# State products moved ahead of the diagonal and carried blocks of a Mamba-2 layer, and VectorE's weighting of x ahead of its gate

## The reference, cut to what matters

```python
states = jnp.einsum('bclh,bclhn,bclhp->bchpn', decay_states * dt_c, B_c, x_c)
def step(prev, inp):
    st, cd = inp
    new = cd[:, :, None, None] * prev + st
    return (new, prev)
Y_off = jnp.einsum('bclhn,bchpn,bclh->bclhp', C_c, prev_states, state_decay_out)
yh = (Y_diag + Y_off).reshape(b, l, H, P) + D_param[None, None, :, None] * x
hidden = yr * jax.nn.silu(gate)
hidden = hidden * lax.rsqrt(var + EPS) * norm_w
return hidden @ out_proj_w
```

## Time and profile before

| | |
|---|---|
| three runs | 1876.63, 1875.66, 1876.63 us, median 1876.63 |
| profiled execution | 1876.75 us, of which 1875.0 us from the first to the last instruction |
| busy share of the span | TensorE 99%, VectorE 80%, ScalarE 66%, GpSimd 44% |
| granted TensorE clock, mean | 0.999 of full speed |
| pair stage | four times some 230 us, between the attention parts |

### The profile page before, as it was taken

One profiled execution on the slowest core, in us unless ns is written; L12 is line 12 of the kernel. 1 busy time (PEld: TensorE's weight loads), 2 busy tenths in 40 slices (PEclk: granted clock), 3 DMA queues, 4 the chain that ended last, 5 costly groups with the idle time before them and its releaser, 6 DMA issues.

```text
span 1875.0 us, 42153 instructions
## 1 busy us (share of the span) xinstructions
PE 1852.3 (99%) x12602; PEld 1574.3 (84%) x12602; DVE 1500.1 (80%) x2736; ACT 1237.9 (66%) x2867; POOL 828.0 (44%) x1005
## 2 busy tenths in 40 slices
PE   8999999999999999999999999999999999999998
PEld 7888778888888878888888887888888888788886
DVE  6886778888788468888888846988888883688886
ACT  5663489999455247888755525888865551588885
POOL 2210379998200027777710002777770000277776
PEclk9999999999999999999999999999999999999999
DMA  6330478887422125656622212656652321366663
GB/s 242 126 126 1 158 231 264 259 265 240 144 78 89 54 82 194 209 205 218 210 98 79 77 54 82 227 205 206 217 189 90 91 66 54 117 215 205 207 215 112
DMA packets 157193, 290.76 MB, mean 155 GB/s; under 512 B 12944, under 2 KB 83792, under 8 KB 157008
## 3 DMA queue, kind: packets, MB, share of 16 engines
q1 hardware_dynamic: 157136, 290.04, 46.6%
HBM read 248.70 MB, written 38.14 MB: 153 GB/s over the span
## 4 chain that ended last, share of the span: by engine, by line
PE 92%; DVE 3%; ACT 2%; issue 1%; POOL 1%; DMA 0%; SPq 0%; POOLq 0%; DVEq 0%; ACTq 0%
PE bank L745 40%; PE bank L1047 11%; PE bank L1034 7%; PE bank L1014 6%; PE both L745 5%; PE bank L863 4%; PE bank L1023 4%; PE bank L1006 3%; PE bank L912 2%; PE bank L831 1%; PE bank L837 1%; PE both L863 1%; PE bank L753 1%; PE bank L750 1%; PE bank L751 1%
## 5 line engine op out<-in xcount | busy, mean ns | idle before, releaser
L745 PE MATMUL bank<-xn_r,w_r 128*128 128x512 f32 x2268 | 566.6, 398 | 0.9 <-DVE xn_r L1738 0.9
L745 PEld LDWEIGHTS bank<-xn_r,w_r 128*128 128x128 f32 x2268 | 412.6, 188 | 83.6 <-issue 1.1
L1510 DVE SCALAR_TENSOR_TENSOR conv_acc<-bank,conv_sb,conv_acc 128x511 f32<-128x511 f32 (+2 forms) x408 | 304.0, 745 | 44.7 <-DVE conv_acc L1510 17.3
L605 POOL TENSOR_TENSOR rstd<-var_eps,minus_half 128x4 f32<-128x4 f32 (+2 forms) x12 | 9.7, 807 | 603.8 <-DVE var_eps L1439 603.8
L1047 PE MATMUL bank<-wo_n,place 128*128 128x256 f32 x1024 | 242.4, 380 | 2.3 <-DVE place L1687 2.3
L626 POOL TENSOR_TENSOR c_grow<-c_grow,c_t 128x768 f32<-128x768 f32 x128 | 234.0, 1828 | 22.5 <-DVE place L1519 22.5
L1159 ACT ACTIVATE place_r<-bank 128x512 fp32r<-128x512 f32 (+1 forms) x320 | 158.7, 556 | 120.6 <-PE bank L745 96.0
L1426 DVE TENSOR_TENSOR place_r<-bank,place_r 128x512 fp32r<-128x512 f32 (+1 forms) x320 | 186.3, 630 | 63.6 <-ACT place_r L1159 63.6
L1047 PEld LDWEIGHTS bank<-wo_n,place 128*128 128x128 f32 x1024 | 184.8, 190 | 22.8 <-DVE place L1687 2.7
L648 POOL TENSOR_TENSOR sumsq<-sumsq,place 128x512 f32<-128x512 f32 x127 | 162.0, 1276 | 17.0 <-ACT place L1227 17.0
L1238 ACT ACTIVATE conv_acc<-bank,conv_sb 128x512 f32<-128x512 f32 x136 | 105.7, 778 | 89.2 <-PE bank L745 85.3
(11 more groups left out here) (174 smaller groups left out, 3544.8 us busy)
## 6 DMA issues: line engine op xcount, KB each, us to landing
place_r<-cum_rows SPq DMA_DIRECT2D x128, 512.0 KB, 4.3
c_grow<-grow_rows SPq DMA_DIRECT2D x128, 384.0 KB, 3.5
w_r<-pair_split SPq DMA_DIRECT2D x96, 512.0 KB, 3.7
w_r<-qkv_split SPq DMA_DIRECT2D x48, 512.0 KB, 4.0
pair_split<-w_r SPq DMA_DIRECT2D x32, 512.0 KB, 3.4
qkv_split<-w_r SPq DMA_DIRECT2D x16, 768.0 KB, 3.9
w_r<-qkv_split SPq DMA_DIRECT2D x48, 256.0 KB, 3.2
wo_n<-out_split SPq DMA_DIRECT2D x96, 128.0 KB, 2.0
```

Source lines behind the costliest of these rows:

```text
L745: ins = mm(out, lhsT=w(a), rhs=m(b), start=(start and i == 0), stop=(stop and i == 2), **kw)
L1510: stt(out=conv_acc[:, back:W], in0=src[:, 0:W - back], scalar=conv_sb[:, ch, TAPS - 1 - back:TAPS - back], in1=conv_acc[:, back:W], op0=AL ...
```

## The change

On TensorE, make_states(n+1) moves from the end of the pair to right behind project_out(n-1), so that in_block(n) and off_block(n) come last. On VectorE, weighted(n+1) is issued before pair_gate(n+1). ScalarE, GpSimd and SP keep their orders, and no semaphore or buffer changes.

```diff
                     if before > 0:
                         project_out(b, n - 1, 1 - par, isinstance(n, int) and n == 1, False)
+                    if more:
+                        make_states(b, n + 1, 1 - par)
                     in_block(b, n, par)
                     off_block(b, n, par)
-                    if more:
-                        make_states(b, n + 1, 1 - par)
...
                     mixed(b, n, par)
                     if more:
+                        weighted(b, n + 1, 1 - par)
                         pair_gate(b, n + 1, 1 - par)
-                        weighted(b, n + 1, 1 - par)
                         if ahead:
                             conv_taps(K + n + 4, n + 2 if isinstance(n, int) else bass.ds(n + 2, 1), bank[1])
```

## The result

| | before | after |
|---|---|---|
| median | 1876.62 us | 1936.55 us (1934.61 to 1936.92) |
| ratio | | 1.0319, 95% interval 1.0302 to 1.0335 |
| span of the profiled execution | 1875.0 us | 1935.1 us |
| mean granted clock | 0.999 | 0.999 |
| looped pair, mean distance of in_block's starts, 1720 to 1840 us | 7.487 us | 7.949 us |

What follows compares the result with a forecast made beforehand. TensorE was taken as the bound, with nothing waiting in the loop. 120 looped pairs at +0.45 us (54.0), first pairs 6.5 and the end 0.7 add 61.2 to 1876.75: 1938 us, 3.3% slower, range 1903 to 1970.

Steps and rivals of the forecast that it cites:

- The state products would stand for weigh_x: In looped pairs behind project_out, TensorE would idle about 0.5 us before the state products' weight loads.
- L: Hand-over latencies from turn_x through weighted and weigh_x to the state products: 0.35 us a pair, bounds 0.12 and 0.55.
- operands picked by a register: In the loops, instructions picking columns by register can start later; turn_x to weighted taken as 0.11 us, bounds 0.03 and 0.2.
- W: Gaps at tile changes, state products to in_block 0.24 us and off_block to next gate projection 0.17: 0.41, bounds 0 and 0.73.
- the rule L + W - 0.31: Change in us per looped pair: +0.45 forecast, -0.19 with low bounds, +0.97 with high ones.
- worth up to 0.16 us a pair to the new order: At tile changes on TensorE, the price goes with the preceding matmul, favouring the new order by up to 0.16 us a pair.
- Free tile changes: Rival: tile changes cost nothing in the new places, +0.04 us a pair, about 1887 us (1880 to 1912); chance 0.12.
- The rival on the other side: Rival: the chain hides after all and the shorter gap stays as gain, 1859 us at -0.19 a pair; chance 0.04.
- A second late party: Rival: conv_end, mixed or ScalarE late, or gaps and latencies at upper ends; +0.75 to +0.97 a pair, 1976 to 2002; chance 0.10.
- The granted clock: Rival: TensorE's clock falls to 1.2 GHz because it stands 0.5 us each pair, about 2040 us; chance 0.03.
- pair 0: First pair of each sequence, no output projection before the state products, chain bare: +1.63 us, four times, 6.5 us.
- the end: In the last sequence the last output projections wait for gated behind the final off_block: +0.7 us.

Runs made afterwards that it cites:

- experiment 4: Changed kernel, but state products read x weighted by dt alone, decay to the chunk's end left out, so nobody waits for weigh_x; 1877.69 us, ratio 1.0008.
- turn_late: Against the kernel before: turn_x moved behind project_out, state products still last, VectorE issuing weighted before pair_gate; 1922.57 us, ratio 1.0250.
- experiment 3: Changed kernel with the state products moved between in_block and off_block, VectorE as in the changed kernel; 1918.11 us, ratio 1.0223.
- experiment 8: Against the kernel before: turn_x behind project_out, gate projection n+2 between off_block and the state products, VectorE in its old order; 1876.38 us, ratio 1.0002.
- Experiments 6 and 9: 6 is turn_late; 9 is experiment 8 with VectorE's weighted before pair_gate, 1922.72 us, ratio 1.0249.
- experiment 2: Against the kernel before: only TensorE's move, state products behind project_out, with pair_gate still before weighted on VectorE; 1983.2 us, ratio 1.0570.

## Why the prediction was right

**The state products would stand for weigh_x: right.** About 0.5 us forecast from the pair's own rows, 0.60 to 0.62 measured before the weight loads in looped pairs (0.58 in sequence 0); without anyone waiting for weigh_x the loss is gone (experiment 4). Three experiments changed the chain's length and the time followed (table above).

**The chain's terms: right, L slightly small.** L was taken as 0.35. In the pair shown it is 0.16 + 0.20 + 0.05 = 0.41. The chain from turn_x's end to the state products is 1.93 us, forecast 1.86. Where L comes from shows in pair 1, which is written out and not looped. There turn_x ends at 1684.77:

```profile
1684.81 0.69 DVE L1543 TENSOR_TENSOR place<-bank,dt_sb 128x512 f32<-128x512 f32 x1 [0.18 <-PE bank L1006]
...
1685.58 0.83 POOL L619 TENSOR_TENSOR shared<-place,dec 128x384 f32<-128x384 f32 x1 [0.33 <-DVE place L1543]
...
1686.46 0.74 PEld L1014 LDWEIGHTS bank<-shared,b_sb 128*128 128x128 f32 x6 [0.37 <-POOL shared L619]
```

The three hand-overs are 0.04, 0.08 and 0.05 us, 0.17 in all and 0.24 less than in the loop, and the state products stand 0.37 us instead of 0.61. VectorE is not what makes the first one longer in the loop: in turn_late, where it stands idle for 1.00 us, the hand-over is 0.17 too (1792.03 to 1792.20). So being in the loop adds 0.24 us a pair to this chain, in its first two hand-overs. The prediction's reason, operands picked by a register, fits, but nothing here isolates it. For the first hand-over the prediction took 0.11, between the 0.03 outside and the loop's unknown value, and most of the 0.06 by which L fell short is here.

**The tile changes, W: the total near, the reasoning wrong.** From the state products' start to the next gate projection I had 2.18 + 0.41 = 2.59; measured 1773.88 to 1776.43 (1774.75 + 0.82 + 0.69 + 0.17), 2.55, so W is 0.37. The gap before in_block is 0.13 us, forecast 0.17. With the measured L and W the rule L + W - 0.31 gives +0.47 a pair, and 0.46 was measured: it holds while the chain sets the pace. But the statement that the price goes with the matmul in front, "worth up to 0.16 us a pair to the new order", is false, and with it the gain that the rule promised below 0.31: W alone is more, and without a wait the new order gains 0.02. The gap in front of a tile change was read as its price; it also holds streaming that is due in any order. What a change costs is 0.16 us (experiment 3), 0.19 by the distances in experiment 8. The Trainium skill ("TensorEngine Tiling (Array Packing)", section "Tiling Modes") says that each change of mode drains TensorE. The runs fit that: the time goes with the number of changes, and not with what stands in front of them.

**The rivals.** Free tile changes are out: two more of them cost 0.32 us a pair (experiment 3), and from the state products to the next gate projection the pair took 0.37 us more than the 2.18 without a gap. The rival on the other side, a chain that hides after all, is out by the 124 waits. A second late party did not come in this change: conv_end ran from 1770.27 to 1770.95, and turn_x's loads started at 1771.12, 0.17 us of room where I had named 0.1. Experiments 6 and 9 show what it costs when VectorE is the late one. The granted clock stayed at 0.999 though TensorE's weight loads stand 0.6 us in every pair, and at 0.998 with about 1.0 us (experiment 2). The warning of the Trainium skill ("TensorE: Matmul & The Clock Gate", section "A second HAM failure mode: psum-queue depth-cycling"), that brief pauses between groups of matmuls can let the clock swing, did not come true for pauses of this length.

**The sum: right as a whole, with some luck.** The looped pairs grew by 7.949 - 7.487 = 0.46 us, forecast 0.45. L was 0.06 too small and W 0.04 too large, so the two errors nearly cancelled. The rest can be counted from turn_x to turn_x. The pairs behind pair 0 grew by 53.9 us together, forecast 54.0: 0.46 each in the loops of the last three sequences, 0.43 in sequence 0, mostly a little less in pair 1 and in the last ones. Pair 0 was mis-sized. Its next gate projection came 1.59 us later, forecast 1.63, but in the kernel before the turn_x behind it had stood for conv_end, 0.58 us in sequence 0 and 0.17 to 0.20 in the others:

```profile
252.20 0.42 PEld L1006 LDWEIGHTS bank<-ident,place 128*128 128x128 f32 x4 [0.58 <-DVE place L1519]
```

That wait is gone in the changed kernel, so pair 0 cost 1.06 us once and 1.43 three times, 5.3 together where I had 6.5. With 0.7 for the end the sum is 59.9. The spans differ by 60.1 us and the medians by 59.9, forecast 61.2.

One reading of the rows was loose. The 124 gaps before the state products are 120 of 0.17 us and, once a sequence, 0.33 before the very first ones; pair 0's state products waited for weigh_x even before the change. No term of the sum hangs on it.

## What to carry to other kernels

A step fed by a chain over other engines (here TensorE, VectorE, GpSimd, TensorE) needs, between the chain's start and itself, more of its own engine's work than the chain is long. Add the durations and the hand-overs before moving it: three of them took 0.4 us inside this loop and 0.2 outside. Here x_w lay ready 1.15 us early. The move took away 2.0 us of cover (from project_out's end to the old start of the state products), and VectorE's swap gave some 0.4 back.

Don't take an idle gap beside a change of tile or behind wide matmuls as its price. Compare the distance between the starts of the same group in two orders.

The order of two steps on one engine was worth 47 us, nothing, -13 and -46 us in four orders of TensorE. The step whose input is ready first should be served first, and which one that is changes when another engine's order changes.

## What the runs showed of the hardware

A pair of this loop takes TensorE 7.47 to 7.49 us in three different orders with two tile changes each, and 7.81 us with four. One change between 128x128 and 128x64 tiles costs 0.16 us of the pair in this stream of float32 matmuls; by the starts of the groups beside it the cost is 0.19 us, behind 256 columns and behind 128 alike.

A wait of 0.61 us before weight loads costs 0.48 us (7.949 against 7.467); the first 0.1 us or so of it costs nothing. TensorE restarts without a further price that shows, and its granted clock stays at 0.999.

From the end of one engine's work to the start of the next: TensorE to VectorE 0.04 us outside the loop and 0.16 inside, VectorE to GpSimd 0.08 and 0.20, GpSimd to TensorE's weight loads 0.05 in both.
